# Relu on ScalarE, two additions on GpSimd, and new numbers for the list scheduler in a fused vision tower on one core

## What is computed

```python
h = patchify(x) @ tok_W.T + tok_b                    # 768 -> 192
# block 1, on n = layernorm(h): a selective state-space layer and a gated FFN
z = (r @ W_in.T) * sigmoid(r @ W_gate.T)             # r = rmsnorm(n) * w, 192 -> 384
dt_in, B, C = split(z @ W_xproj.T)
dt = softplus(dt_in @ W_dt.T + b_dt)
state = scan(exp(dt * A), (dt * z) * B)              # 16 states per channel, over the tokens
y = (state * C).sum(states) + D_skip * z
y1 = n + y @ W_out.T
h = h + y1 + (silu(f @ W_gate_ffn.T) * (f @ W_up.T)) @ W_down.T   # f = rmsnorm(y1) * w
# block 2, on n = layernorm(h): 16 experts, the best 4 per token
t = rmsnorm(n) * scale
w = softmax(top4(t @ gate_w.T + gate_b))
e = swiglu(t @ w1 + b1) @ w2 + b2                    # for every expert, 192 -> 384 -> 192
h = h + n + sum(w * e)
```

## Time and profile before

| | us |
|---|---|
| runs | 654.14, 652.72, 653.54 |
| median | 653.54 |
| profiled execution, its own time | 651.45 |
| its span, first to last instruction | 649.6 |
| TensorE busy | 571.8 |
| VectorE busy | 481.3 |
| GpSimd busy | 378.0 |
| ScalarE busy | 290.3 |

### The profile page before, as it was taken

The page is one execution under the profiler, slowest core; times in us unless marked ns, Lnnn a source line. Parts: engine busy times, 40 slices in busy tenths (PEclk is TensorE's granted clock), DMA queues, the critical chain, the costliest instruction groups (busy, mean ns, idle before and its releaser), DMA issues.

```text
span 649.6 us, 10399 instructions
## 1 busy us (share of the span) xinstructions
PE 571.8 (88%) x3361; PEld 488.8 (75%) x3361; DVE 481.3 (74%) x922; ACT 290.3 (45%) x684; POOL 378.0 (58%) x437
## 2 busy tenths in 40 slices
PE   4957879896799999789999997799998899987996
PEld 3746668784699999568888875688886788866785
DVE  1162886899877877997787799978898866556664
ACT  1154766455544444464534463554442343233342
POOL 3354696675456545656665556676666465453674
PEclk8665958996899999899999997999999799996999
DMA  9784240713046342204533520354442165542872
GB/s 260 272 283 146 73 147 3 265 74 146 3 112 214 92 164 87 80 2 138 178 109 103 174 77 13 93 150 172 141 150 86 34 200 195 187 171 47 278 249 73
DMA packets 41826, 88.34 MB, mean 136 GB/s; under 512 B 9580, under 2 KB 34476, under 8 KB 35500
## 3 DMA queue, kind: packets, MB, share of 16 engines
q1 hardware_dynamic: 41772, 87.68, 41.3%
HBM read 77.24 MB, written 10.40 MB: 135 GB/s over the span
## 4 chain that ended last, share of the span: by engine, by line
PE 62%; DVE 17%; issue 5%; ACT 5%; DMA 4%; POOL 3%; SPq 2%; DVEq 0%; POOLq 0%; ACTq 0%
PE post L768 13%; PE sums L768 11%; PE gate_up L768 9%; PE linear_up L768 9%; PE y_sum L768 9%; PE pre L768 8%; DVE state L1258 5%; DVE fills L1249 3%; PE fills L768 3%; DMA scratch<-expert_w 3%; DVE dts L1225 2%; DMA w<-w_store 1%; POOL read L1466 1%; ACT scratch L1033 1%; DVE scratch L1364 1%
## 5 line engine op out<-in xcount | busy, mean ns | idle before, releaser
L1466 POOL TENSOR_TENSOR read<-state,c_all 128x504 f32<-128x504 f32 (+1 forms) x120 | 145.6, 1217 | 119.2 <-DVE state L1258 86.0
L1258 DVE TENSOR_TENSOR_SCAN state<-a_bar,fills 128x504 f32<-128x504 f32 (+1 forms) x120 | 133.2, 1110 | 11.2 <-POOL read L1466 2.1
L768 PE MATMUL y_sum<-read,ident 128*128 128x252 f32 (+1 forms) x480 | 129.6, 399 | 7.9 <-POOL read L1466 4.5
L1485 POOL TENSOR_TENSOR scratch<-scratch 128x252 f32<-128x252 f32 (+1 forms) x120 | 81.4, 679 | 93.8 <-DVE scratch L1379 88.5
L1033 ACT ACTIVATE scratch<-scratch 128x252 f32<-128x252 f32 (+1 forms) x120 | 47.5, 396 | 156.3 <-DVE scratch L1364 156.1
L768 PE MATMUL sums<-hid,w 128*128 128x252 f32 (+1 forms) x480 | 102.5, 374 | 4.4 <-POOL hid L1494 4.4
L768 PEld LDWEIGHTS y_sum<-read,ident 128*128 128x128 f32 x480 | 90.8, 213 | 20.5 <-issue 4.9
L1033 ACT ACTIVATE a_bar<-dts,decay 128x245 f32<-128x245 f32 (+1 forms) x240 | 99.7, 470 | 4.2 <-DVE dts L1233 2.9
L768 PE MATMUL gate_up<-t_high,w 128*128 128x252 f32 (+1 forms) x360 | 88.7, 316 | 5.6 <-DVE logits L1324 2.2
L768 PE MATMUL linear_up<-t_high,w 128*128 128x252 f32 (+1 forms) x360 | 86.0, 309 | 7.2 <-ACT mix_w L1033 6.4
L1364 DVE TENSOR_SCALAR scratch<-gate_up,vec 128x252 f32<-128x252 f32 (+1 forms) x120 | 54.4, 453 | 50.9 <-PE gate_up L768 49.8
(11 more groups left out here) (166 smaller groups left out, 875.3 us busy)
## 6 DMA issues: line engine op xcount, KB each, us to landing
w<-w_store SPq DMA_DIRECT2D x40, 1152.0 KB, 5.6
route_rows<-mix_rows SPq DMA_DIRECT2D x192, 63.0 KB, 3.0
w_store<-w SPq DMA_DIRECT2D x8, 1152.0 KB, 5.0
scratch<-expert_w SPq DMA_DIRECT2D x16, 384.0 KB, 5.8
w<-expert_w SPq DMA_DIRECT2D x1, 2304.0 KB
route_rows<-mix_rows SPq DMA_DIRECT2D x48, 36.0 KB, 2.8
w_embed<-embed_w SPq DMA_DIRECT2D x3, 256.0 KB, 3.6
x_patch<-patches SPq DMA_DIRECT2D x1, 756.0 KB, 6.0
```

Source lines behind the costliest of these rows:

```text
L768: return nc.tensor.matmul(out, lhsT, rhs, start=start, stop=stop, skip_group_check=shared, is_transpose=turned)
L1258: dve.tensor_tensor_scan(pair(state, i, c), pair(a_bar, i, c), pair(fills, i, c), 0.0, ALU.mult, ALU.add).then_inc(scanned.sem, 1)
L1466: pool.tensor_tensor(by_state(pair(read, i, c)), by_state(pair(state, i, c)), c_all[:, n:n + 2, 0:tok(c)], ALU.mult).then_inc(read_out.sem, 1)
L1485: pool.tensor_tensor(glu[:, 0:tok(c)], product[un % 2][:, 0:tok(c)], g_one[un % 2][:, 0:tok(c)], ALU.mult)\
```

## The change

Relu moves from VectorE (`delta_max`, which is gone) into ScalarE's `delta_abs`; the second addition of `h1` and the whole of `t_low` move from VectorE to GpSimd, where they take their turn in the same `ORDER`. The turns and `needed()` lose `delta_max`. In the planner, the time from one engine to the next is no longer one `HOP` but a `LATENCY` of the engine that hands over, the engines are first free at other times, most `COST` entries have new values, and the weight and the spans are new.

```diff
@@ before_scan, needed
-              [("bc_low", 0), ("delta", 0), ("delta_abs", 0)], [("delta_max", 0)], [("delta", 1), ("delta_abs", 1)],
-              [("delta_max", 1), ("delta_exp", 0), ("factor", 0)]]
+              [("bc_low", 0), ("delta", 0), ("delta_abs", 0)], [("delta", 1), ("delta_abs", 1)],
+              [("delta_exp", 0), ("factor", 0)]]
-        return [(0, "delta_max", 1)] if c == 1 else []
+        return [(0, "delta_abs", 1)] if c == 1 else []
@@ schedule, lay
-    free = {e: 0.0 for e in "PVSG"}
+    free = {"P": 4.0, "V": 4.0, "S": 10.0, "G": 4.0}
-                start = max(at[engine], ready + HOP)
+                start = max(at[engine], ready)
-                at[engine] = ready = start + us * (0.25 + 0.75 * size)
+                at[engine] = start + us * (0.25 + 0.75 * size)
+                ready = at[engine] + LATENCY[engine]
@@ COST (those that changed most)
-    "delta_abs": (("S", .7),), "delta_max": (("V", .7),), "poly": (("V", .9),), "log1p": (("V", .9),),
+    "delta_abs": (("S", 1.2),), "poly": (("V", .7),), "log1p": (("V", .72),),
-    "decay": (("S", .95),), "drive_b": (("V", .67),), "advance": (("V", 1.2),), "read": (("G", 1.25),),
+    "decay": (("S", .82),), "drive_b": (("V", .6),), "advance": (("V", 1.13),), "read": (("G", 1.2),),
-    "h1": (("V", 1.2),), "t_low": (("V", .7),), "x_gate": (("P", .57),), "x_linear": (("P", .57),),
+    "h1": (("V", .55), ("G", 1.25)), "t_low": (("G", 1.25),), "x_gate": (("P", .6),), "x_linear": (("P", .6),),
-    "x_min": (("V", .45),), "x_low": (("V", .45),), "x_gated": (("V", .55),), "x_down": (("P", .43),),
+    "x_min": (("V", .43),), "x_low": (("V", .41),), "x_gated": (("V", .34),), "x_down": (("P", .47),),
-TWO_PORTS = {"x_gated", "poly", "log1p", "t_low", "bc_low"}
-HOP = 0.12
-WAIT_WEIGHT = 1.4
-BEFORE_SPAN = 18.0
-AFTER_SPAN, LAST_AFTER_SPAN = 18.2, 16.5
-EXPERT_SPAN, LAST_EXPERT_SPAN = 20.8, 24.3
+TWO_PORTS = {"x_gated", "poly", "log1p", "bc_low"}
+LATENCY = {"P": 0.22, "V": 0.12, "S": 0.1, "G": 0.14}
+WAIT_WEIGHT = 0.5
+BEFORE_SPAN = 15.5
+AFTER_SPAN, LAST_AFTER_SPAN = 20.9, 22.0
+EXPERT_SPAN, LAST_EXPERT_SPAN = 25.1, 21.7
@@ ScalarE, delta_abs
                         .then_inc(v_abs.sem, 1)
+                    activate(us[:, c % 2, j, 0:tok(c)], half(pre_of(c), c, j % 2), ACT.Relu, bias=col("dt_b", j))\
+                        .then_inc(v_max.sem, 1)
@@ VectorE
-            def delta_max(c, part):
-                js = (0, 1) if part == 0 else (2,)
-                dve.wait_ge(v_abs.sem, v_abs.at(c, js[-1] + 1))
-                for j in js:
-                    dve.tensor_scalar(us[:, c % 2, j, 0:tok(c)], half(pre_of(c), c, j % 2), col("dt_b", j), 0.0,
-                                      ALU.add, ALU.max).then_inc(v_max.sem, 1)
             def h1(c, _):
...
                 dve.tensor_tensor(y1, y1, both(post, c), ALU.add).then_inc(y2_added.sem, 1)
-                dve.wait_ge(y2_added.sem, y2_added.at(c, 1))
-                dve.tensor_tensor(h0, h0, y1, ALU.add).then_inc(h1_ready.sem, 1)
-            def t_low_rest(c, _):
-                dve.wait_ge(t_high_ready.sem, t_high_ready.at(c, 1))
-                dve.tensor_tensor(t_low[:, :, 0:tok(c)], t_in[:, :, 0:tok(c)], t_high[:, :, 0:tok(c)].bitcast(F32),
-                                  ALU.subtract).then_inc(t_low_ready.sem, 1)
@@ GpSimd
+            def t_low_rest(c, _):
+                pool.wait_ge(t_high_ready.sem, t_high_ready.at(c, 1))
+                pool.tensor_tensor(t_low[:, :, 0:tok(c)], t_in[:, :, 0:tok(c)], t_high[:, :, 0:tok(c)].bitcast(F32),
+                                  ALU.subtract).then_inc(t_low_ready.sem, 1)
+            def h1(c, _):
+                y1, h0 = y1s[:, c % 3, :, 0:tok(c)], h0s[:, c % 3, :, 0:tok(c)]
+                pool.wait_ge(y2_added.sem, y2_added.at(c, 1))
+                pool.tensor_tensor(h0, h0, y1, ALU.add).then_inc(h1_ready.sem, 1)
```

More of the change, by code:

```diff
@@ L340 @@
 COST = {
-    "embed": (("P", .85),), "embedded": (("S", .9),), "mean": (("P", .85),), "center": (("V", .68),),
-    "square": (("S", .62),), "variance": (("P", .9),), "roots": (("V", .3),), "power": (("G", 1.),),
+    "embed": (("P", .87),), "embedded": (("S", .9),), "mean": (("P", .85),), "center": (("V", .6),),
+    "square": (("S", .56),), "variance": (("P", .9),), "roots": (("V", .18),), "power": (("G", 1.),),
     "spread": (("P", .45),), "scale": (("V", 1.5),), "inproj": (("P", 1.7),),
-    "gate": (("S", .36),), "z": (("V", .42),), "xproj": (("P", 1.27),), "dt_in": (("S", .45),),
@@ L345 @@
[L345 to L349, removed]
+    "gate": (("S", .32),), "z": (("V", .38),), "xproj": (("P", 1.27),), "dt_in": (("S", .45),),
@@ L350 @@
+    "bc_copy": (("V", .36),), "bc_high": (("S", .36),), "bc_low": (("V", .4),), "delta": (("P", .65),),
+    "delta_abs": (("S", 1.2),), "delta_exp": (("S", .75),), "factor": (("S", .9),),
+    "poly": (("V", .7),), "log1p": (("V", .72),), "drive": (("G", 2.2),), "c_spread": (("P", .25),),
+    "c_copy": (("S", .52),), "decay": (("S", .82),), "fill": (("P", .25),), "drive_b": (("V", .6),),
+    "advance": (("V", 1.13),), "read": (("G", 1.2),), "collect": (("P", .85),), "y": (("V", .43),),
     "outproj": (("P", 1.27),), "y1_add": (("V", .6),), "square2": (("S", .62),), "variance2": (("P", .9),),
-    "roots2": (("V", .3),), "power2": (("G", 1.),), "spread2": (("P", .23),),
@@ L352 @@
-    "scale2": (("V", .85),), "ffn_up": (("P", 1.7),), "ffn_tanh": (("S", .36),), "ffn_product": (("V", .85),),
-    "down": (("P", 1.7),), "h1": (("V", 1.2),), "mean3": (("P", .85),), "center3": (("V", .68),),
-    "square3": (("S", .62),), "variance3": (("P", .9),), "roots3": (("V", .3),), "power3": (("G", 1.),),
+    "roots2": (("V", .18),), "power2": (("G", 1.),), "spread2": (("P", .23),),
+    "scale2": (("V", .78),), "ffn_up": (("P", 1.7),), "ffn_tanh": (("S", .36),), "ffn_product": (("V", .78),),
@@ L355 @@
+    "down": (("P", 1.7),), "h1": (("V", .55), ("G", 1.25)), "mean3": (("P", .85),), "center3": (("V", .58),),
+    "square3": (("S", .62),), "variance3": (("P", .9),), "roots3": (("V", .18),), "power3": (("G", 1.),),
     "spread3": (("P", .45),), "scale3": (("V", 1.5), ("G", 1.3)),
-    "t_high": (("S", .62),), "t_low": (("V", .7),), "x_logits": (("P", .9),), "x_topk": (("V", 2.2),),
+    "t_high": (("S", .62),), "t_low": (("G", 1.25),), "x_logits": (("P", .9),), "x_topk": (("V", 2.2),),
     "x_exp": (("S", .3),), "x_route": (("V", 1.2),), "x_turn": (("P", .25),), "x_mix": (("S", .7),),
-    "x_start": (("P", .85),), "x_gate": (("P", .57),), "x_linear": (("P", .57),), "x_min": (("V", .45),),
@@ L359 @@
-    "x_tanh": (("S", .36),), "x_one": (("S", .36),), "x_low": (("V", .45),), "x_gated": (("V", .55),),
-    "x_glu": (("G", .7),), "x_scale": (("G", .7),), "x_down": (("P", .43),), "x_finish": (("V", 1.2),),
+    "x_start": (("P", .85),), "x_gate": (("P", .6),), "x_linear": (("P", .6),), "x_min": (("V", .43),),
+    "x_tanh": (("S", .33),), "x_one": (("S", .4),), "x_low": (("V", .41),), "x_gated": (("V", .34),),
+    "x_glu": (("G", .68),), "x_scale": (("G", .68),), "x_down": (("P", .47),), "x_finish": (("V", 1.2),),
@@ L1404, in _ @@
             run({"center": center, "roots": roots, "scale": scale, "z": z_product,
-                 "bc_copy": bc_copy, "bc_low": bc_low, "delta_max": delta_max, "poly": poly, "log1p": log1p,
+                 "bc_copy": bc_copy, "bc_low": bc_low, "poly": poly, "log1p": log1p,
                  "drive": drive, "drive_b": drive_b, "advance": advance, "y": y_block, "y1_add": y1_add,
@@ L1408, in _ @@
                  "center3": center3, "roots3": roots3, "scale3": scale3,
-                 "t_low": t_low_rest, "x_topk": x_topk, "x_route": x_route, "x_min": x_min, "x_low": x_low, "x_gated": x_gated,
+                 "x_topk": x_topk, "x_route": x_route, "x_min": x_min, "x_low": x_low, "x_gated": x_gated,
                  "x_finish": x_finish})
@@ L1512, in _ @@
             run({"scale": scale, "power": power, "power2": power2, "power3": power3, "split_w1": split_w1,
-                 "drive": drive, "read": read_states, "outproj": outproj, "scale3": scale3, "x_glu": x_glu,
+                 "drive": drive, "read": read_states, "outproj": outproj, "scale3": scale3, "h1": h1, "t_low": t_low_rest, "x_glu": x_glu,
                  "x_scale": x_scale})
```

2 lines of the change are left out of this document (1 added, 1 removed).

## The result

The changed kernel takes 627.18 us (median; 626.73 to 630.13) against 653.36 us for the kernel before in the same runs: a ratio of 0.961, 95% interval 0.958 to 0.964. The direction was right, the size was not.

The account below looks back on a forecast made before the run. VectorE was taken to bound four crossings, TensorE three other stretches. Terms: 7.3 + 0.65 + 1.1 - 2.0 + 2.0 = 9 us, so 644.5 us against the 653.54 median (chance 0.42); range 632 to 659 us.

Parts of the forecast that it names:

- these four stretches are VectorE's: Crossings at 140-180, 260-300, 375-420, 485-520 us: VectorE nearly full, TensorE lacks 31.0 us together.
- The relief, 7.3 + 0.65 us: Moved work leaving VectorE: 7.3 us gained in its four stretches, 0.65 us from Relu at 60 to 140 us.
- the port's 2.0: VectorE's stretches: moved operations on GpSimd stop two-input VectorE operations, taking 2 us back; ends 0 and 6.6.
- rival (1): VectorE's stretches: every moved GpSimd operation stops a VectorE one, 6.6 us come back; 649.1 us, chance 0.10.
- rival (2): Whole kernel: VectorE's freed time turns into waits for TensorE, order effects cancel; 653.5 us, chance 0.09.
- The last crossing, 1.1 us: Last cut's routing: without t_low ahead on VectorE, the logits start some 1.1 us earlier; gain 1.1 us.
- The order, net 2.0 us: Crossings: experts under the scan gain 5.4 us; cut 0's later experts cost 1.4, cut 3's lost cover 2.0.
- The closing of the gaps: Crossings at 260 and 375 us: experts run through, half of 10.8 us TensorE idle closes, 5.4 us gained.
- rival (4): Crossings: all 10.8 us of idle close, no port loss, no loss of cover; 635 us, chance 0.18.
- rival (3): Three full TensorE stretches: at wait weight 0.5 steps with late inputs block the queue, 15 us lost; 659.5 us, chance 0.21.
- the lost cover: Crossing of cut 3's experts, moved behind the last scan: 2.0 us lost; ends 0 and 7.3.
- The sign for the forecast: Crossings at 260 and 375 us keep under 4 us of TensorE idle each, experts running through them.

Follow-up runs that it names:

- e1: The kernel before with only the three moves to ScalarE and GpSimd, its planner and order kept: 650.16 us, ratio 0.997.
- e8: The changed kernel with AFTER_SPAN 18.2 and EXPERT_SPAN 20.8 again for the first three cuts: 649.66 us, ratio 0.995.
- e2: The kernel before with the new planner, the three operations left on VectorE, Relu right behind its Abs: 636.33 us, ratio 0.976.
- e10: The kernel before with the new planner, the three operations left on VectorE, Relu just before the step that needs it: 635.78 us, ratio 0.975.
- e12: The changed kernel with WAIT_WEIGHT 1.4 again instead of 0.5: 640.56 us, ratio 0.982.
- e9: The kernel before with only AFTER_SPAN 20.9 and EXPERT_SPAN 25.1 for the first three cuts: 656.45 us, ratio 1.007.
- e14: The kernel before with WAIT_WEIGHT 0.5 and AFTER_SPAN 20.9, EXPERT_SPAN 25.1 for the first three cuts: 641.55 us, ratio 0.984.
- e7: The changed kernel with the low part (t_low) on VectorE again, ahead of the routing steps: 625.72 us, ratio 0.959.

## Why the prediction was wrong

**What bounds the kernel.** Half right. The crossings were the place to look, and the reason was misread: "these four stretches are VectorE's". Freed of 2.0, 1.1 and 0.9 us there, VectorE let TensorE do nothing more (e1); given expert steps to issue, TensorE did 58 and 32 matmuls more beside a VectorE that had shorter operations taken away but more of the experts' to do (the changed kernel against the earlier trace rows). The stretch lacked ready work of the right kind, as e8 shows best: 186 matmuls beside a VectorE busy 29.5 of 40 us.

**The relief, 7.3 + 0.65 us, and the port's 2.0 against it.** Mis-sized under the order it was reckoned in: 2 us (e1), where the sum had 7 with the last crossing. That lies near the 2.45 us that rival (1) leaves for the moves and the nothing of rival (2), and both signs are there in part: VectorE's busy time fell by 10.4 us and not by 16.2, so 5.8 came back, and its waits for `gate_up` and `linear_up` grew by 5.4 us. Under the new order the moves give 8.6 to 9. The prediction took for granted that relief and order add.

**ScalarE.** Right: 15 Relus of 0.45 us, busy 295.2 us against some 297, no second table load. Its reordering was not tested by itself.

**GpSimd and the port.** GpSimd is busy 388.3 us against some 390. The port was put at 2.0 us; with the moves alone VectorE got 5.8 us of its time back, 3.0 of them in `x_gated` (e1), and the order brought another 11 in that group (the changed kernel against e1). VectorE's busy time was therefore 475 and not 465.

**The last crossing, 1.1 us.** The step failed in calling the gate matmuls "not the later branch": they became it by 0.23 us at `x_min`, and `mix_w` stands behind `x_min`'s followers in ScalarE's queue. 0.2 us were gained.

**The order, net 2.0 us.** This is the step that failed: the new order gives 16 to 17 us alone (e2, e10), and about 23 beside the moves (e1 against the changed kernel). The prediction saw rightly that expert matmuls would come under the scan where TensorE starved, and mis-sized it. Its parts:

- The closing of the gaps was taken as half of 10.8 us of TensorE idle; even all of it, rival (4), was too little. Counted in matmuls, the two stretches gained 15 us (an estimate, 90 matmuls at 6 a us), against 8.6 in the idle column. Part of what the column hides is the clock, which rose from 0.91 to 1.00 at 260 to 300 us; at 375 to 420 it stayed at 0.92, and what it hides there is not shown.
- The weight, of which "its sign I can't tell", was put at nothing and was worth 13 us (e12). The range held a price for its loss, rival (3), and none for its gain. With it the dates give 22 us (e8), without it they lose 4 (e9): the sum had no term for that.
- The first 60 us were left out of the rows, and 50 matmuls were gained there.
- The later start of cut 0's experts was sized well: from 60 to 180 us e9, with the new dates alone, issues 518 matmuls against 525, some 1 us, where 1.4 were taken. The end of the last cuts costs more than the 2.0 us taken for the lost cover: behind the last scan TensorE is idle 5.6 us longer than before. How much of that is the cover is open; 3.4 us of it are waits for expert weights.

**Rival (3)**, the looser order, did not come true: in the three full stretches TensorE is idle 5.0 us in all, under the 9 that it asked for (300 to 375 us has 73.8 us busy and 454 matmuls against 463), and the lower weight is a gain as a whole (e12, e14 against e9).

**The sign for the forecast** came nearly true: the crossings at 260 and 375 us keep 2.2 and 4.4 us of TensorE idle, where under 4 each was asked. It says that the gaps closed and not what that is worth.

## What to carry to other kernels

In a pipelined kernel with in-order queues, look for the stretches in which one kind of work is missing, and count instructions done, not only idle time, since a half-clocked or modelled busy engine hides what is lost. Try to spread each stream over the whole period before taking work off the engine that looks full: here dates and weight together gave 10 us with nothing moved, and the offload 2 without them. Do not judge a planner's numbers one at a time: the same dates gave 22 us beside the low weight and lost 4 beside the high one. And when an operation is put back for a test, put it where it is needed, or its place is measured in its stead.

## What was not expected of the hardware

A very small two-input operation of VectorE is held by a GpSimd operation too. The comparison `chosen`, 126x32 with both inputs in SBUF, took 0.71 us beside `t_low`, ending at 562.90 as `t_low` ended at 562.85, against 0.19 us in all five cuts of the kernel before. In the changed kernel it takes 0.69 to 0.76 us in four of five cuts (3.1 us in all against 1.0), and with `t_low` back on VectorE (e7) 0.19 again. The logits' addition of the same size, with one input in PSUM, took 0.19 us beside `base` at 561.04.

At the half clock a matmul takes nearly twice as long. In 10 us of the start-up (50 to 60) TensorE was busy 7.1 us at a granted clock of 0.50 before and 9.0 us at 1.00 after, with 21 and 60 matmuls. The same pair of 128x252 matmuls (`post<-squares,w_in`) took 1.13 us there before (58.05) and 0.59 after (51.15).
